# Local attention of the first block: values with narrow weights on column strips, scores in two rounded one-pass matmuls

## The reference, cut to what matters

```python
def local_attn(q, k, v):                      # heads 0..3, e = 16, WINDOW = 128
    bq = q.reshape(bh, nb, WINDOW, e)
    bk2, bv2 = look_around(bk), look_around(bv)             # previous and own window: 256 keys
    dots = einsum('bwie,bwje->bwij', bq, bk2) * e ** (-0.5)
    dots = where(causal_mask | pad_mask, mask_value, dots)
    attn = softmax(dots, axis=-1)
    out = einsum('bwij,bwje->bwie', attn, bv2)
def causal_linear_attn(q, k, v):              # heads 4..7, BUCKET = 64
    q, k = softmax(q, -1), elu(k) + 1
    k_cum = cumsum(bk.sum(-2), -2)
    ctx = cumsum(einsum('bhund,bhune->bhude', bk, bv), 2) / (k_cum[..., None] + 1e-6)
    ctx = one bucket later (the first bucket sees zero)
    out = einsum('bhund,bhude->bhune', bq, ctx)
def self_attention(x, Wq, Wk, Wv, Wo, bo):
    out = concatenate([lo, go], axis=1)  ->  out @ Wo + bo
for i in range(4):
    x = x + self_attention(layer_norm(x), ...)
    x = x + gelu(layer_norm(x) @ W1 + b1) @ W2 + b2
```

## Time and profile before

| | us |
|---|---|
| median of 3 runs | 3130.52 (3129.12 to 3149.68) |
| profiled execution | 3123.45 |
| its span | 3121.7, mean granted TensorE clock 0.963 |
| PE busy | 2882.0 (92%) |
| DVE busy | 1969.7 (63%) |
| ACT busy | 1873.3 (60%) |
| POOL busy | 965.9 (31%) |

### The profile page before, as it was taken

One profiled execution on the slowest core, in us unless ns is written; L12 is line 12 of the kernel. 1 busy time (PEld: TensorE's weight loads), 2 busy tenths in 40 slices (PEclk: granted clock), 3 DMA queues, 4 the chain that ended last, 5 costly groups with the idle time before them and its releaser, 6 DMA issues.

```text
span 3121.7 us, 58985 instructions
## 1 busy us (share of the span) xinstructions
PE 2882.0 (92%) x21844; PEld 2000.2 (64%) x21844; DVE 1969.7 (63%) x5736; ACT 1873.3 (60%) x4388; POOL 965.9 (31%) x812
## 2 busy tenths in 40 slices
PE   8999999987999999879999999899899898998997
PEld 5767675743888888548888888555445464554554
DVE  5445454536677777568878787677377424764774
ACT  5464646541466666227767777577577533875774
POOL 1010101010232332025555555255255212552551
PEclk9999999988799999889999999999999999998999
DMA  1010000000000000100000000221021001210210
GB/s 51 1 39 1 12 1 9 1 4 8 1 2 2 2 2 2 50 22 2 2 2 2 2 2 2 90 54 42 13 60 45 1 22 45 51 36 13 57 41 14
DMA packets 35263, 62.85 MB, mean 20 GB/s; under 512 B 11526, under 2 KB 15654, under 8 KB 33830
## 3 DMA queue, kind: packets, MB, share of 16 engines
q1 hardware_dynamic: 34982, 59.07, 6.9%
HBM read 23.48 MB, written 1.15 MB: 8 GB/s over the span
## 4 chain that ended last, share of the span: by engine, by line
PE 78%; DVE 7%; ACT 6%; issue 3%; POOL 3%; SPq 2%; DMA 1%; DVEq 0%; POOLq 0%; ACTq 0%
PE bank L766 67%; PE bank L984 5%; PE bank L1099 3%; SPq L732 2%; POOL work L1869 2%; PE bank L836 1%; ACT work L1217 1%; DVE work L1583 1%; ACT bank L1225 1%; ACT squared L1227 1%; ACT work L1338 1%; DVE work L1727 1%; ACT squared L1324 0%; DVE low L1640 0%; DVE normed L1465 0%
## 5 line engine op out<-in xcount | busy, mean ns | idle before, releaser
L766 PEld LDWEIGHTS bank<-work 128*64 128x64 f32 (+3 forms) x4992 | 418.3, 163 | 186.0 <-issue 140.2
L766 PE MATMUL bank<-work 128*64 128x128 f32 (+8 forms) x4992 | 518.9, 291 | 18.4 <-ACT work L1217 8.7
L1302 ACT ACTIVATE low<-bank,low 128x512 f32<-128x512 f32 (+23 forms) x384 | 227.4, 592 | 339.2 <-DVE low L1640 335.5
L1217 ACT ACTIVATE low<-bank 128x512 f32<-128x512 f32 (+3 forms) x512 | 425.4, 941 | 1.7 <-PE bank L984 1.7
L766 PE MATMUL bank<-table_keys,halves 128*128 128x512 f32 (+3 forms) x1536 | 422.1, 384 | 0.8 <-ACT low L1302 0.8
L1640 DVE TENSOR_REDUCE low<-bank 128x1 f32<-128x512 f32 (+22 forms) x512 | 288.8, 572 | 167.2 <-PE bank L766 161.8
L1217 ACT ACTIVATE work<-bank 128x512 f32<-128x512 f32 (+5 forms) x469 | 246.8, 546 | 155.2 <-PE bank L766 59.6
L1830 POOL TENSOR_TENSOR halves<-squared,const 128x512 fp32r<-128x512 f32 x128 | 135.5, 1059 | 570.6 <-PE bank L766 570.5
L1788 POOL TENSOR_SCALAR normed<-normed,slot 128x512 f32<-128x512 f32 x48 | 75.4, 1571 | 703.4 <-DVE normed L1465 703.1
L766 PEld LDWEIGHTS bank<-table_keys,halves 128*128 128x128 f32 x1536 | 248.8, 194 | 56.8 <-issue 33.8
L1338 ACT ACTIVATE work<-work 128x192 f32<-128x192 f32 (+1 forms) x512 | 218.8, 431 | 46.7 <-DVE work L1720 46.7
(11 more groups left out here) (195 smaller groups left out, 5630.9 us busy)
## 6 DMA issues: line engine op xcount, KB each, us to landing
work<-work SPq DMA_DIRECT2D x512, 64.0 KB, 2.0
slot<-in_wW SPq DMA_DIRECT2D x4, 1605.5 KB, 6.8
slot<-in_wA SPq DMA_DIRECT2D x4, 837.0 KB, 6.1
table_low<-embv_padded SPq DMA_DIRECT2D x2, 1536.0 KB, 6.3
table<-in_dft SPq DMA_DIRECT2D x1, 3072.0 KB, 12.6
slot<-in_wE SPq DMA_DIRECT2D x2, 584.0 KB, 3.7
const<-in_const SPq DMA_DIRECT2D x1, 1094.0 KB, 5.3
squared<-in_x SPq DMA_DIRECT2D x4, 256.0 KB, 6.3
```

The lines of the kernel that those rows point to most:

```text
L766: return pe.matmul(o, l, r, start=start, stop=stop)
L1217: return act.activation(dst, src, ACT.Identity)
L1302: act.activation(PR[t.G % 4][:, 0:n], bank[t.G % 2][:, 0:n], ACT.Exp, bias=NBR[:, t.G % 4:t.G % 4 + 1], accum_out=RSR[:, t.G % 8:t.G % 8 + ...
```

## The change

- The local q and k are laid out twice (`twice_each`): rows 32h to 32h+15 and 32h+16 to 32h+31 both hold head h. ACT rounds q and k to float32r (`Q_HI`, `K_HI`). DVE forms `Q_BOTH`, which is q itself on the first 16 rows and q minus its rounded value on the second 16 (`low_rows` is 0 or -1), and `K_LO`, k minus its rounded value. ACT copies `Q_BOTH` into the four planes of `QL`, now float32r and 32 rows each, after waiting for DVE (`a_q_split`).
- `a_scores` makes two float32r matmuls per head (`QL` by `K_HI`, `QL` by `K_LO`), two heads to a bank.
- The softmax is divided on POOL (`a_weigh`, after a reciprocal on DVE that waits for the exponentials) before the transposes; `SA` is gone, `PA` has three buffers.
- `a_values` has `TM` (128x16) as the stationary and `TA` (128 columns) as the moving operand; head h goes to partitions 32h of one bank that is held for the four windows of a lane (banks 6 and 7 in turn; other steps of the attention loop have banks 0 to 5). The context of the linear heads is a 64x128 stationary operand and comes first. The result is feature-major, so `a_out` needs no transposes; ACT copies the bank once (`a_heads`), `Wo`'s rows are reordered on the host.
- In a turn the plan now has `a_scores(i)`, `a_values(i-2)`, then the steps by `w`, then `a_weigh(i)` and `a_turn(i-1)`.

```diff
@@ make_plan, stage_a
+            state["pool"] = SHORT
@@
-                if 1 <= i <= C * NT:
-                    add("a_turn", c=(i - 1) // NT, w=(i - 1) % NT, i=i - 1)
                 if 2 <= i <= C * NT + 1:
-                    add("a_values", c=(i - 2) // NT, w=(i - 2) % NT, i=i - 2)
+                    if (i - 2) % NT == 0:
+                        held = add("a_values", c=(i - 2) // NT, w=0, i=i - 2)
+                    else:
+                        add("a_values_on", c=(i - 2) // NT, w=(i - 2) % NT, i=i - 2, tile=held)
+                    if (i - 2) % NT == NT - 1:
+                        add("a_heads", c=(i - 2) // NT, tile=held)
...
+                if i < C * NT:
+                    add("a_weigh", c=c, w=w, i=i)
+                if 1 <= i <= C * NT:
+                    add("a_turn", c=(i - 1) // NT, w=(i - 1) % NT, i=i - 1)
+            state["pool"] = range(BANKS)
@@ tensor
             def a_scores(s):
...
+                pe.wait_ge(sem("a_k_split"), s.n // NT + 1)
                 for h in range(LOC):
-                    mm(take(s.k + h)[:, lo:256], QL[:, b, h, s.w * P:(s.w + 1) * P],
-                       KL[:, b, (s.w - 1) * P + lo:(s.w + 1) * P]).then_inc(tile_full, 1)
+                    if h % 2 == 0:
+                        o = take(s.k + h // 2)
+                    for keys_ in (K_HI, K_LO):
+                        last = mm(o[:, 256 * (h % 2) + lo:256 * (h % 2) + 256], QL[:, b, h, s.w * P:(s.w + 1) * P],
+                                  keys_[:, b, (s.w - 1) * P + lo:(s.w + 1) * P], start=(keys_ is K_HI), stop=(keys_ is K_LO))
+                    if h % 2:
+                        last.then_inc(tile_full, 1)
             def a_turn(s):
-                pe.wait_ge(sem("a_exp"), s.n + 1)
+                pe.wait_ge(sem("a_weighed"), s.n + 1)
+            def window_values(s, o, n):
...
+                pe.wait_ge(sem("a_context_done"), lane + 1)
+                pe.wait_ge(sem("a_q_turned"), lane + 1)
+                for u in (2 * s.w, 2 * s.w + 1):
+                    mm(o[:, u * BUCKET:(u + 1) * BUCKET], CN[0:64, u].rearrange("p h a d -> p (h a d)"),
+                       QT[0:64, u * BUCKET:(u + 1) * BUCKET], start=(u == 2 * s.w), stop=False)
+                pe.wait_ge(sem("a_turned_act"), n + 1)
+                pe.wait_ge(sem("a_turned_dve"), n + 1)
+                for blk in range(0 if s.w else 1, 2):
+                    for h in range(LOC):
+                        last = mm(o[32 * h:32 * h + DH_A, s.w * P:(s.w + 1) * P],
+                                  TM[:, b, s.w - 1 + blk, P + h * DH_A:P + (h + 1) * DH_A],
+                                  TA[:, i, h // 2, (2 * (h % 2) + blk) * P:(2 * (h % 2) + blk + 1) * P],
+                                  start=False, stop=(blk == 1))
             def a_out(s):
-                pe.wait_ge(sem("a_normalised"), NT * (s.n + 1))
-                for w in range(NT):
-                    last = pe.transpose(o[:, w * P:(w + 1) * P], ON[:, b, w, :], ident)
                 pe.wait_ge(sem("a_heads"), s.n + 1)
@@ scalar, a_project
-                for h in range(LOC):
-                    r = slice(32 * h, 32 * h + DH_A)
-                    copy(QL[r, b, h, :], full(s.k)[r, :]).then_inc(sem("a_local_copied"), 1)
-                copy(KL[:, b, :], full(s.k + 1)[:, :]).then_inc(sem("a_local_copied"), 1)
+                copy(Q_HI[:, b, :], full(s.k)[:, :]).then_inc(sem("a_rounded"), 1)
+                copy(K_HI[:, b, :], full(s.k + 1)[:, :]).then_inc(sem("a_rounded"), 1)
+                act.wait_ge(sem("a_q_split"), s.n + 1)
+                for h in range(LOC):
+                    r = slice(32 * h, 32 * h + 32)
+                    copy(QL[r, b, h, :], whole_words(Q_BOTH[r, b, :])).then_inc(sem("a_local_copied"), 1)
@@ scalar
+            def a_heads(s):
+                act.wait_ge(sem("a_valued"), (NT - 1) * (s.n + 1))
+                copy(AT, tile_of(s.tile.k)[:, :]).then_inc(sem("a_heads"), 1)
@@ vector, a_project
+                dve.wait_ge(sem("a_rounded"), 2 * s.n + 1)
+                dve.scalar_tensor_tensor(out=Q_BOTH[:, b, :], in0=whole_words(Q_HI[:, b, :]), scalar=k_("low_rows"),
+                                         in1=full(s.k)[:, :], op0=ALU.mult, op1=ALU.add).then_inc(sem("a_q_split"), 1)
+                dve.wait_ge(sem("a_rounded"), 2 * s.n + 2)
+                dve.tensor_tensor(K_LO[:, b, :], full(s.k + 1)[:, :], whole_words(K_HI[:, b, :]), ALU.subtract)\
+                    .then_inc(sem("a_k_split"), 1)
@@ vector
-            def a_values(s):
-                link(dve.reciprocal(inverse, small_a[:, 4 + s.i % 4, 0:LOC]))
-                dve.tensor_tensor(ON[:, b, s.w, 0:64]..., o[:, 0:64]..., bc(inverse.unsqueeze(2), [P, LOC, DH_A]), ALU.mult)
-                dve.tensor_copy(ON[:, b, s.w, 64:128], o[:, 64:128]).then_inc(sem("a_normalised"), 1)
+            def a_weigh(s):
+                dve.wait_ge(sem("a_exp"), s.n + 1)
+                dve.reciprocal(small_a[:, 8 + s.i % 4, 0:LOC], small_a[:, 4 + s.i % 4, 0:LOC]).then_inc(sem("a_inverted"), 1)
@@ gpsimd
+            def a_weigh(s):
+                lo = 0 if s.w else P
+                pool.wait_ge(sem("a_inverted"), s.n + 1)
+                row = PA[:, s.i % 3, :, lo:256]
+                pool.tensor_tensor(row, row, bc(small_a[:, 8 + s.i % 4, 0:LOC].unsqueeze(2), [P, LOC, 256 - lo]), ALU.mult)\
+                    .then_inc(sem("a_weighed"), 1)
```

More of the change, by code:

```diff
@@ L124 @@
     "norm_scale": (("norm_rstd", 1, 1),),
-    "a_project": (("a_local_copied", LOC + 1, LOC), ("a_local_copied", LOC + 1, LOC + 1)) + each("a_token_copied", 2),
+    "a_project": (("a_q_split", 1, 1), ("a_k_split", 1, 1)) + each("a_token_copied", 2),
     "a_context": (("a_q_turned", 1, 1), ("a_context_read", 1, 1)),
-    "a_scores": each("a_scored", LOC),
+    "a_scores": (("a_scored", LOC, 2), ("a_scored", LOC, 4)),
     "a_turn": (("a_turned_act", 1, 1), ("a_turned_dve", 1, 1)),
-    "a_values": (("a_normalised", 1, 1),),
-    "a_out": (("a_heads", 1, 1),) + STREAM,
+    "a_values": (("a_heads", 1, 1),),
+    "a_out": STREAM,
     "a_mlp": each("a_gelu", 4) + STREAM,
@@ L182, in add @@
         for name, a, b in LAST_READ.get(kind, ()):
-            b_ = min(HELD if kind == "w_values" else state["pool"], key=lambda one: (newest[one], one))
+            b_ = min(HELD if kind in ("a_values", "w_values") else state["pool"], key=lambda one: (newest[one], one))
             banks.append(b_)
@@ L516, in hybrid_network @@
         cursor[0] = max(cursor[0], 8192)
-        QL = carve(2, LOC, T)
+        CN = carve(NB_A, LOC, 2, DH_A)
+        QL = table_keys[:, :].rearrange("p (a h t) -> p a h t", a=2, h=LOC)
+        place = [halves, WORK_W - LOW]
+        cursor[0] = 0
+        K_HI, K_LO = carve(2, T), carve(2, T)
+        cursor[0] = 4096
+        Q_HI, Q_BOTH = carve(2, T), carve(2, T)
+        place = [work, WORK_W]
         HB = work[:, 0:8192].rearrange("p (a b c) -> p a b c", a=4, b=4)
-        CN0 = CN
         cursor[0] = 0
@@ L838, in a_turn @@
                     last.then_inc(tile_full, 1)
-            def a_values(s):
-                i, b = s.i % 2, s.c % 2
-                pe.wait_ge(sem("a_turned_act"), s.n + 1)
-                pe.wait_ge(sem("a_turned_dve"), s.n + 1)
-                o = take(s.k)
-                for h in range(LOC):
-                    for blk in range(0 if s.w else 1, 2):
-                        mm(o[:, h * DH_A:(h + 1) * DH_A],
-                           TA[:, i, h // 2, (2 * (h % 2) + blk) * P:(2 * (h % 2) + blk + 1) * P],
-                           TM[:, b, s.w - 1 + blk, P + h * DH_A:P + (h + 1) * DH_A],
-                           start=(blk == (0 if s.w else 1)), stop=(blk == 1))
-                pe.wait_ge(sem("a_context_done"), s.n // NT + 1)
-                pe.wait_ge(sem("a_q_turned"), s.n // NT + 1)
-                for e in range(2):
-                    u = 2 * s.w + e
-                    last = mm(o[64 * e:64 * e + 64, 64:128], QT[0:64, u * 64:(u + 1) * 64], CN[0:64, u, :])
-                last.then_inc(tile_full, 1)
@@ L858, in a_out @@
-            def a_out(s):
-                b = s.c % 2
-                pe.wait_ge(sem("a_normalised"), NT * (s.n + 1))
-                o = take(s.k)
-                for w in range(NT):
-                    last = pe.transpose(o[:, w * P:(w + 1) * P], ON[:, b, w, :], ident)
-                last.then_inc(tile_full, 1)
+            def window_values(s, o, n):
+                i, b = s.i % 2, s.c % 2
+                lane = n // NT
+                pe.wait_ge(sem("a_context_done"), lane + 1)
[11 more added lines that the diff above has]
+                                  start=False, stop=(blk == 1))
+                return last
@@ L1243, in a_scores @@
             def a_scores(s):
-                i, lo = s.i % 2, (0 if s.w else P)
+                i, lo = s.i % 3, (0 if s.w else P)
                 for h in range(LOC):
                     act.wait_ge(sem("a_scored"), LOC * s.n + h + 1)
```

(7 more changed lines are left out.)

61 lines of the change are left out of this document (30 added, 31 removed).

## The result

The changed kernel takes 3045.28 us (median of 4 runs, 3039.37 to 3053.55) where the kernel before took 3138.0 beside it (4 runs): a ratio of 0.9704, interval 0.9659 to 0.975, some 93 us faster by the ratio. The profiled span went from 3121.7 to 3037.6 us, 84 less. The forecast was 3064 within 3008 to 3106, faster with 0.8. Since the kernel before was at 3138.0 beside it and not at 3130.5, the gain itself was forecast 25 us too small, 68 for 93. Most of the mechanism held too, but which of its parts earn the gain came out otherwise (experiments 2, 3 and 9).

A forecast was written before the change was run, and what follows sets the result against it. PE was taken to bound the kernel, with 78% of the chain that ended last. Gains of 32.8 less losses of 15.9 left 16.9 us per layer, 68 in four, from 3130.5 to 3063, rounded to 3064; range 3008 to 3106.

The forecast's parts named there:

- scores: PE's local attention scores: one-pass matmuls save 0.60 us per full window, 7.2 us per layer.
- values, with the pause: PE's value matmuls on four strips: 0.035 us a record, 0.24 us per window added for a pause; gain 14.5 us per layer.
- wait for `AT`: PE's output projection waiting for ACT's copy: hidden for three of four lanes, gain 5.9 us per layer.
- clock behind it: Projection and next scores running slow after a wait for `AT`: 1.5 us per layer gained, once.
- values wait for copies: PE's values waiting for DVE's late copy of the transposes: new loss of 13.5 us per layer.
- start of the layers: Scores at a layer's start wait for q rounded, split and copied instead of copied: loss 0.9 us per layer.
- last window, POOL: The last window's chain through POOL is not covered: loss 1.5 us per layer.
- the walk: One lane traced from PE's start of w=2: PE ready at 9.2 us, DVE's copy done at 11.05, wait 1.9.
- A: Rival: DVE's lateness is hidden, only 2.4 us at the ends remain; 122 us gain, 3009 us; chance 0.17.
- B: Rival: POOL's weighing chain ends last too; 23 us lost gives 3087, 58 lost gives 3121, no change (chance 0.13).
- C: Rival: each value step waits for DVE, 2.3 us per turn, and the clock falls; slower, 3195 us; chance 0.05.
- D: Rival: strips do not overlap with 16 columns, the values' 14.5 us per layer go; about 3100 us; chance 0.07.

The follow-up runs named there:

- experiment 2: The kernel before with only the split of q and k and the one-pass scores; 3151.02 us, ratio 1.0029.
- experiment 3: The changed kernel with float32 scores and the old five copies of q and k; 3047.43 us, ratio 0.9706 to the kernel before.
- experiment 9: The changed kernel with ACT's copy into `AT` moved back directly before the output projection; 3113.96 us, ratio 0.9918 to the kernel before.
- experiment 4: The changed kernel with all heads' value matmuls on partitions 0 to 15, one strip; 3097.56 us, ratio 0.9871 to the kernel before.
- experiment 6: The changed kernel without POOL's weighing product, transposes waiting for the exponentials alone; 3032.86 us, ratio 0.9675 to the kernel before.
- exp. 12: The plan of experiments 10 with float32 scores, no rounding and no split; 3038.89 us, ratio 0.9684 to the kernel before.
- experiment 8: The kernel of experiment 2 with four one-pass score matmuls per head instead of two; 3198.03 us, ratio 1.0197 to the kernel before.
- exp. 5: The changed kernel with `a_values` in turns w=0, 2 and 3 moved behind the turn's other steps; 3038.74 us, ratio 0.9688 to the kernel before.
- exp. 7: The changed kernel with `a_turn(i-1)` placed before `a_weigh(i)`; 3059.43 us, ratio 0.975 to the kernel before.
- experiments 10: The kernel of exp. 5 with, from layer two, the first turn's two norm steps before the layer's first scores; 3044.12 us, ratio 0.9702.
- experiment 11: The kernel of experiments 10 with two of the four `Q_BOTH` copies made by POOL instead of ACT; 3044.34 us, ratio 0.9698 to the kernel before.

## Why the prediction was right, and where it was not

The terms in us over the four layers, gains positive:

| term | forecast | measured in stage A |
|---|---|---|
| scores | 28.8 | 30.4 |
| values, with the pause | 58.0 | 66.8 - 21.3 - 2.9 = 42.6 |
| transposes of `ON` and their wait | 14.8 | 11.9 + 2.8 = 14.7 |
| wait for `AT` | 23.6 | 26.4 - 2.8 = 23.6 |
| clock behind it | 6.0 | about 5, all other forms |
| values wait for copies | -54.0 | -26.7 |
| start of the layers | -3.6 | 6.8 - 10.6 = -3.8 |
| last window, POOL | -6.0 | 0.6 - 1.5 = -0.9 |
| sum | 68 | 85 by groups, which overlap a little; 80.3 by the end of stage A |

That the sum is not further off is partly luck: errors of both signs stand in it, the values 15 us too good, their waits 27 us and POOL's 5 us too bad. (The sum itself gives 3062.5, which the prediction rounded up twice, to 3064.)

**Scores, right in size, wrong in what they were worth.** Eight one-pass matmuls take 1.19 to 1.20 us; less the last one's own 0.30, seven steps are 0.13 us each, inside the 0.13 to 0.15 that was named. But experiment 3 gives the whole gain without them. What the forecast did not ask is whether this term and the debit of 13.5 us per layer for the values' waits belong together. They do: with the one-pass scores the waits are 6.7 us per layer, with the old ones 1.9.

**Values: the term that was too large, by 15 us.** A record is 0.042 us where the earlier trace rows gave 0.035, and "The context's two matmuls keep four records; I take no change" failed: 0.66 us per window instead of 0.33. Where 0.24 us per window was set aside for a pause, these 0.33 and 0.05 of idle time came. Whether its stationary operand of 128 columns or the change of tile shape costs this is open: the form costs the same in experiment 4 (41.6 us). The Trainium skill ("TensorE: Matmul & The Clock Gate", measured speedup against the span model) gives 2.38 times for three column tiles, by which a record would be an estimated 0.049 us. The measured 0.042 lies in the middle between this and the row's 0.035; four strips took 2.9 times less than one (experiment 4).

**Values wait for DVE's copy: the right wait, half the size.** This is the step that put the forecast too high. DVE and PE from the scores of one turn w=2 to the values of w=3, changed kernel:

```profile
208.31 1.19 PE L779 MATMUL bank<-halves,table_keys 128*128 128x256 f32 x8
...
212.88 0.75 DVE L1504 SCALAR_TENSOR_TENSOR halves<-halves,const,bank 128x512 fp32r<-128x512 f32 x1 [1.59 <-ACT halves L1237]
213.55 0.69 DVE L1507 TENSOR_TENSOR halves<-bank,halves 128x512 fp32r<-128x512 f32 x1
...
214.16 0.68 DVE L1511 COPY work<-bank 128x512 f32<-128x512 f32 x1
...
214.76 0.68 DVE L1511 COPY work<-bank 128x512 f32<-128x512 f32 x1
215.47 0.42 DVE L1516 TENSOR_REDUCE work<-work 128x16 f32<-128x256 f32 x1
...
216.47 0.74 DVE L1470 SCALAR_TENSOR_TENSOR inner<-bank,slot,inner 128x512 f32<-128x512 f32 x1
...
217.13 0.17 DVE L1563 RECIPROCAL work<-work 128x4 f32<-128x4 f32 x1
217.22 0.66 DVE L1557 COPY work<-bank 128x512 f32<-128x512 f32 x1
...
218.03 0.63 PE L779 MATMUL bank<-work 128*16 128x128 f32 x16 [0.51 <-DVE work L1557]
```

From the scores of w=2 at 208.31 the walk had PE ready 9.2 us later; it is ready at 217.52, which is 9.2. It had the copy done after 11.05; it is done after 9.6. Each of the wide DVE instructions lasts 0.68 to 0.75 us, but where its successor stands ready that one starts 0.60 to 0.67 us after it. Their records overlap by some 0.08 us, and the walk added whole durations, with a hop of 0.2 us between engines that is 0.15 here from the copy to PE (217.88 to 218.03). Over a dozen of them, and with ACT's rounding done some 0.4 earlier, that makes about the 1.4 us between 1.9 and 0.51.

In the whole of layer two the values' waits are 1.23, 0.51 and 0.53 us in w=3 (forecast 1.9 each), 0.45, 0.45 and 0.54 in w=0 (1.15 each), 0.53, 0.53 and 1.40 in w=1 (0.9 each) and 0.69 once in w=2 (0.4 four times). That is 6.9 us, and 6.7 per layer on average, not 13.5; and the longest stand at the layer's start and end, not in its middle. All of w=0 and the 1.23 wait for ACT's copy of the transposes and not for DVE's: over stage A 10.6 of the 26.7 us. For DVE's copy alone, which the forecast named, it is 4.0 us per layer.

**The output's wait: exact as a term, and the weight of it missed.** 23.6 us was forecast and 23.6 is gone, yet putting the copy back costs 62 us of stage A (experiment 9): in the new kernel this wait is longer (3.53 us for 2.61) and brings the clock down more often (behind seven of twelve, for three of eight). The forecast priced the clock behind it at 6 us, from a kernel with float32 scores.

**The rivals.** A (waits hidden) asked for less than 4 us per layer and got 6.7, so it is refuted; but the gain of 93 us lies about midway between its 122 and the forecast's 68, and of DVE's copy alone the waits stand at its bound. B, with its 23 or 58 us, is refuted by 1.5 us of waits behind POOL; experiment 6 leaves room for less than that. C is refuted as named, but its mechanism, waits that lower the clock, is what makes experiment 9 slow. D is refuted by 0.042 us a record, and experiment 4 shows what it would have cost. Attention of layer two took 101.90 us, forecast 104.

**The clock, by the runs.** Time at half clock in stage A, one profile each:

| | wait for `AT` exposed | hidden |
|---|---|---|
| float32 scores | 54.6 (before) | 23.9 (exp. 3), 17.1 (exp. 12) |
| one-pass scores | 160.4 (exp. 2), 146.8 (exp. 8), 116.1 (exp. 9) | 37.5 and 61.4 (the change), 41.0 (exp. 5), 20.5 (exp. 6), 54.6 (exp. 7, 10, 11), 13.7 (exp. 4) |

With the wait hidden one-pass scores mostly stand higher, but the ranges overlap. The clearest pair is experiments 10 and 12, one plan: the mean granted clock of the whole execution is 0.959 to 0.961 in the four runs with one-pass scores and 0.965 to 0.968 in the four with float32 ones. With the wait exposed one-pass scores are at 116 us and more against 54.6, and only these three kernels go over 62. (The 54.6 us are of an execution of 3123.45 us, faster than every other run of the kernel before.)

The left column does not name one cause. Experiment 9 differs from the change in the exposed copy alone, and there the clock falls behind the waits. Experiments 2 and 8 differ from it also in the old form of the values, and in experiment 2 the clock does not fall behind the long waits for `AT`: the stretches that begin with PE busy make up 78 of the 160 us. So two things are shown: in the old kernel the one-pass scores lower the clock (experiment 2), and in the new one the exposed wait does (experiment 9). Whether the old form of the values is what experiment 2 needs was not tried, nor were the new values with float32 scores and the late copy. By what a busy PE loses its clock stays open.

The Trainium skill ("TensorE: Matmul & The Clock Gate", the HAM clock gate) says that idling gates the clock and sustained work releases it. The timeline of experiment 9 agrees. The stretches of experiment 2 that begin with PE busy (clock 1.00, then 0.64) do not, nor does it by itself say why doubling the one-pass work left the clock at 0.90 in experiment 8.

## What to carry to other kernels

A change of two halves should be costed as its halves. Here the half with the column strips and the earlier copy had the whole gain (experiment 3): taking back the strips lost 49 us of it and taking back the copy 63 to 67, losses that overlap, and neither was tried alone on the kernel before. Making the scores' matmuls one-pass gave nothing, since what PE saved came back as waits for the other engines and as clock. When PE's work shrinks, ask of each wait on the same turn how much of that work was its cover. And price a wait on PE with the clock behind it, for the kernel as it will be: the same small copy was worth 29 us of stage A by its waits and 62 in the end.

## What the runs showed of the hardware

- Matmuls with a 128x128 stationary operand and 16 moving columns and their transposed form (16 stationary, 128 moving columns) cost about the same while the outputs share a strip (0.117 and 0.121 us a record); in four strips in turn it is 0.042.
- A wide DVE instruction that stands ready behind another of its own queue starts some 0.08 us before that one's recorded end (214.76 for 214.84 and 213.55 for 213.63 in the changed kernel), so chains are to be read from starts, not summed from durations.
- POOL's copy of 32x512 takes 0.61 us, ACT's 0.63: equal here (experiment 11, L1907 614 ns, L1245 630 ns).
- The granted clock of a stage with PE over 90% busy can be 0.88 (experiment 2), and matmuls that made it 49 us longer did not raise it above 0.90 (experiment 8).
- The clock can fall while PE is busy without a break: 5.00 of 5.00 us from 250 to 265 us of experiment 2, with the granted clock at 1.00, 1.00 and 0.64; and it can stay up behind a wait of 2.72 us, as it did there eight times of eight.
